# Moving gate-times-bias to GpSimd, loading the biases in rows and reordering the projection of a fused attention and feed-forward block

## What is computed

```
xn  = layernorm(x)
qkv = xn @ w_qkv.T + b_qkv              # 32 heads of 16
s   = softmax(q k^T / 4 + alibi, causal) @ v
s   = s @ w_out.T + b_out
g   = silu(ffn(xn))                     # ternary octonion weights: gate, up (1360 wide), down
out = x + s * g
```

## Time and profile before

| | |
|---|---|
| median of 3 runs | 840.68 us (839.41 to 840.71) |
| the profiled execution | 836.7 us, span 834.9 |
| TensorE busy | 796.8 us (95%) |
| VectorE busy | 631.0 us (76%) |
| ScalarE busy | 472.5 us (57%) |
| GpSimd busy | 132.6 us (16%) |
| first projection matmul | at 16.09 us |
| issue of `b_col`, of `bv_row` | at 1.25 us, at 5.11 us |
| end of the last feed-forward tile | at 402.7 us |
| first score matmul | at 406.48 us |
| granted TensorE clock | 1.2 GHz from 407.7 to 414.5 us, else 2.4 |

### The profile page before, as it was taken

The page is one execution under the profiler, slowest core; times in us unless marked ns, Lnnn a source line. Parts: engine busy times, 40 slices in busy tenths (PEclk is TensorE's granted clock), DMA queues, the critical chain, the costliest instruction groups (busy, mean ns, idle before and its releaser), DMA issues.

```text
span 834.9 us, 16148 instructions
## 1 busy us (share of the span) xinstructions
PE 796.8 (95%) x5926; PEld 350.6 (42%) x5926; DVE 631.0 (76%) x1774; ACT 472.5 (57%) x631; POOL 132.6 (16%) x183
## 2 busy tenths in 40 slices
PE   5999999999999999999899999999999999999998
PEld 3444544444444444444343343343433344343333
DVE  6656877743533565664799999999999999996546
ACT  5434285333132232222488888888888788887540
POOL 4223132223032131131000000000000003530000
PEclk9999999999999999999899999999999999999999
DMA  7474322348202201101121122222125233653635
GB/s 264 131 214 165 137 91 77 113 124 299 104 1 76 76 1 38 63 1 41 62 63 60 58 72 80 80 67 79 55 66 166 81 91 107 198 144 116 215 138 219
DMA packets 71056, 88.40 MB, mean 106 GB/s; under 512 B 26926, under 2 KB 37166, under 8 KB 70464
## 3 DMA queue, kind: packets, MB, share of 16 engines
q1 hardware_dynamic: 70848, 87.10, 32.2%
q0 software_dynamic: 128, 0.27, 0.2%
HBM read 51.15 MB, written 35.93 MB: 104 GB/s over the span
## 4 chain that ended last, share of the span: by engine, by line
PE 70%; DVE 16%; DMA 5%; issue 4%; ACT 3%; POOL 1%; SPq 0%; DVEq 0%; ACTq 0%
PE psum L1537 12%; PE psum L1494 9%; PE psum L1560 9%; PE psum L1561 9%; DVE mx L1207 8%; PE psum L1571 5%; PE psum L1572 5%; PE psum L1512 4%; DVE mshown L1203 3%; PE psum L1388 2%; PE psum L1390 2%; PE psum L1389 2%; DMA q_scr<-qk_stage 2%; PE psum L1521 2%; PE psum L1596 1%
## 5 line engine op out<-in xcount | busy, mean ns | idle before, releaser
L922 ACT ACTIVATE probs<-psum,exp_scale 128x1024 f32<-128x1024 f32 (+1 forms) x320 | 310.3, 1028 | 71.3 <-PE psum L1521 51.1
L1203 DVE CUSTOM_DVE_ANT_0 mshown<-psum,ahead 128x384 bf16<-128x384 f32 (+3 forms) x512 | 220.3, 487 | 2.8 <-PE psum L1494 0.4
L1494 PE MATMUL psum<-QKs 51*128 51x512 f16 (+3 forms) x768 | 186.2, 333 | 16.0 <-DVE mx L1207 6.3
L1537 PE MATMUL psum<-probs,Vs 128*32 128x512 f32 (+3 forms) x1536 | 162.3, 511 | 0.2 <-ACT probs L922 0.2
L1207 DVE TENSOR_REDUCE mx<-psum 128x1 f32<-128x512 f32 x256 | 157.6, 681 | 3.3 <-PE psum L1494 2.4
L1512 PE MATMUL psum<-QKs 53*128 53x512 f16 (+3 forms) x768 | 139.0, 331 | 1.6 <-ACT probs L922 1.4
L1560 PE MATMUL psum<-X,room 128*128 128x512 f16 (+1 forms) x352 | 133.6, 379 | 0.0
L1561 PE MATMUL psum<-X,room 128*128 128x512 f16 (+1 forms) x352 | 133.4, 379 | 0.0
L1494 PEld LDWEIGHTS psum<-QKs 51*128 51x128 f16 x768 | 52.1, 93 | 152.0 <-DVE mx L1203 78.9
L954 ACT ACTIVATE room<-psum,gate_half 128x512 f32<-128x512 f32 (+1 forms) x44 | 30.2, 687 | 101.2 <-PE psum L1561 101.2
L800 POOL TENSOR_TENSOR room<-room 128x512 f16<-128x512 f32 (+1 forms) x44 | 50.9, 1156 | 172.2 <-ACT room L959 172.2
(11 more groups left out here) (162 smaller groups left out, 922.1 us busy)
## 6 DMA issues: line engine op xcount, KB each, us to landing
o_scr<-osum SPq DMA_DIRECT2D x32, 256.0 KB, 3.2
QKs<-q_scr SPq DMA_DIRECT2D x96, 64.0 KB
QKs<-k_scr SPq DMA_DIRECT2D x96, 64.0 KB
q_scr<-qk_stage SPq DMA_DIRECT2D x16, 256.0 KB, 2.4
k_scr<-qk_stage SPq DMA_DIRECT2D x16, 256.0 KB, 2.2
v_scr<-v_stage SPq DMA_DIRECT2D x16, 256.0 KB, 2.1
Vs<-v_scr SPq DMA_DIRECT2D x16, 256.0 KB
probs<-in_L_attn_x SPq DMA_DIRECT2D x4, 1024.0 KB, 11.6
```

Of the source, the lines that this page charges most:

```text
L922: nc.scalar.activation(probs[n % PSLOTS][:, 2 * pair:2 * pair + 2, 0:COLS[n]], s_bank[pair][:, :, 0:COLS[n]], ACT.Exp, scale=exp_scale[:, ...
L1203: last = nc.vector.tensor_tensor_reduce(out=mshown[tiles_read(at) % 2][:, cols], in0=m_bank[bank][:, cols], in1=ahead[:, CH - keys:], scal ...
L1494: last = nc.tensor.matmul(tile[:, hh, :], Qs[s][rows, pair + hh, qb * P:(qb + 1) * P], Ks[s][rows, pair + hh, k0:k0 + keys], start=(hh == ...
L1537: last = nc.tensor.matmul(pv_bank[32 * h:32 * h + 32, CH - cols:CH], Vs[s][:, kb, h::QH], probs[n % PSLOTS][:, h, at:at + cols], start=(kb ...
```

## The change

Six edits:

1. y is made by GpSimd. VectorE scales `bo_row` once by `down_half`; then, per token tile, GpSimd multiplies `g_stage` by `bo_row` and adds x. VectorE waits, before it writes a `g_stage` buffer again, for the product of two tiles before.
2. The bias comes as 12 rows of 128, TensorE transposes it into bank 7, ScalarE copies it to `b_col` and takes its squares ahead of the first root. `bv_row` is issued by SyncE behind the weight loads.
3. GpSimd waits for the first normalisation before the three memsets.
4. In the projection: the squares of the value weights ahead of four weight pieces on ScalarE; their sum on TensorE after tile 1, not 2; the scales of the output weights at tile 1, not 2, of the second chunk; the normalisation of the second chunk one to two tiles sooner, its root at tile 2, not 4; in the third chunk the placements of w_down after tiles 2, 3, 5, 6, not 4 to 7.
5. The first batch of maximum tiles in the feed-forward stage holds one tile, not three, so that the last has three, not four; the batches in between are cut accordingly.
6. In the first quad the first score tile stands ahead of the maximum tiles.

```diff
-        if due - given >= MRING or n + 1 == len(tiles):
+        if due - given >= (MRING if given else len(early) % MRING or MRING):
...
+        if t == 0:
+            pieces.sort(key=lambda w: w != ("scores", 0, 0, 0))
...
+        DOWN_AT = [2, 3, 5, 6]
...
-        LN_AT = [[2, 3, 4, 5, 6], [2, 3, 4, 5, 6], [1, 2, 2, 3, 4]]
-        ROOT_AT = [4, 4, 2]
+        LN_AT = [[1, 2, 2, 3, 4], [2, 3, 4, 5, 6], [1, 2, 2, 3, 4]]
+        ROOT_AT = [2, 4, 2]
...
+            sp.dma_start(bv_row[:], b_qkv[2 * D:3 * D].partition_broadcast(P)).then_inc(bv_loaded, 16)
             next_x(1)
...
-            pool.dma_start(b_col[:], b_qkv.rearrange("(t p) -> p t", p=P), allow_slow_non_contiguous=True).then_inc(bias_loaded, 16)
+            pool.dma_start(b_rows[:], b_qkv.rearrange("(t p) -> t p", p=P)).then_inc(bias_loaded, 16)
...
+            pool.wait_ge(ln_step, LN_STEPS)
             for i in range(SLOTS):
                 nc.gpsimd.memset(Vs[i][:, :, QH * HD:], 1.0 / QK_SCALE).then_inc(v_ones, 1)
...
+            def gate_bias(j, t):
+
+                d = j * TT + t
+                if d == 0:
+                    pool.wait_ge(bo_ready, 1)
+                if d >= 2:
+                    pool.wait_ge(y_stored[d % 2], d // 2 * 16)
+                pool.wait_ge(f_evac, j * FTILES + 2 * HT + t + 1)
+                nc.gpsimd.tensor_tensor(y_stage[d % 2], g_stage[d % 2], bo_row[:], ALU.mult).then_inc(y_step, 1)
+                if t == 0:
+                    pool.wait_ge(x_rows_loaded[j], 16)
+                pool.wait_ge(y_step, d + 1)
+                nc.gpsimd.tensor_tensor(y_stage[d % 2], y_stage[d % 2], x_rows[j][:, t, :], ALU.add).then_inc(y_done, 1)
...
+            act.wait_ge(bias_turned, 1)
+            nc.scalar.activation(b_col[:], banks[7][:, 0:3 * KT], ACT.Copy).then_inc(bias_copied, 1)
+            act.wait_ge(bias_copied, 1)
+            for i in range(3):
+                at = SQUARES[i][1] - 1
+                nc.scalar.activation(bsquares[:, i * KT:(i + 1) * KT], b_col[:, i * KT:(i + 1) * KT], ACT.Square, accum_out=wsum[:, at:at + 1]).then_inc(squared, 1)
             root_of(0)
...
             squares(1)
+            squares(2)
             for kt in range(KT):
                 high_weight(KT + kt)
-            squares(2)
...
-                    if c == 2 and m >= NTT:
-                        place_down(m - NTT)
+                    if c == 2 and m in DOWN_AT:
+                        place_down(DOWN_AT.index(m))
...
-                    if c == 1 and m == 2:
+                    if c == 1 and m == 1:
                         out_scales()
...
+                if d == 0:
+                    dve.wait_ge(bo_loaded, 16)
+                    nc.vector.tensor_scalar(bo_row[:], bo_row[:], down_half[:, 0:1], None, ALU.mult).then_inc(bo_ready, 1)
                 if d >= 2:
                     dve.wait_ge(g_stored[d % 2], d // 2 * 16)
+                    dve.wait_ge(y_step, d - 1)
                 nc.vector.scalar_tensor_tensor(out=g_stage[d % 2], in0=held, scalar=1.0, in1=f_bank(tile), op0=ALU.add, op1=ALU.mult).then_inc(f_evac, 1)
-                if d == 0:
-                    dve.wait_ge(bo_loaded, 16)
-                if d >= 2:
-                    dve.wait_ge(y_stored[d % 2], d // 2 * 16)
-                dve.wait_ge(f_evac, tile + 1)
-                nc.vector.scalar_tensor_tensor(out=y_stage[d % 2], in0=g_stage[d % 2], scalar=down_half[:, 0:1], in1=bo_row[:],
-                                               op0=ALU.mult, op1=ALU.mult).then_inc(y_step, 1)
-                if t == HT:
-                    dve.wait_ge(x_rows_loaded[j], 16)
-                dve.wait_ge(y_step, d + 1)
-                nc.vector.tensor_tensor(y_stage[d % 2], y_stage[d % 2], x_rows[j][:, t - HT, :], ALU.add).then_inc(y_done, 1)
...
             pe.wait_ge(s_const, IDENTITY)
+            pe.wait_ge(bias_loaded, 16)
+            nc.tensor.transpose(banks[7][:, 0:3 * KT], b_rows[:], identf[0:3 * KT, 0:3 * KT]).then_inc(bias_turned, 1)
...
-                    if c == 0 and m == 2:
+                    if c == 0 and m == 1:
                         sum_squares(2)
-                    if c == 1 and m == 2:
+                    if c == 1 and m == 1:
                         sum_squares(3)
```

17 lines of the change are left out of this document (10 added, 7 removed).

## The result

The changed kernel takes 831.04 us (median of 4 runs, 829.66 to 832.83) against 840.04 for the one before (838.57 to 840.71): ratio 0.990, 95% interval 0.987 to 0.992, so 9.0 us less (intervals in brackets behind a ratio are 95% intervals throughout). Two repetitions gave 831.16 against 840.24 (0.989, 0.987 to 0.991) and 831.16 against 839.38 (0.990, 0.987 to 0.993). The direction was as forecast; the size was not: 835.7 was forecast, and 831.04 lies under the range of 832.6 to 839.3.

The account below looks back on a forecast made before the run. TensorE bounds the fourth chunk and feed-forward, VectorE's maxima the attention; only start, holes and handover can move. 1.2 + 0.7 + 1.6 + 0.9 + 0.6 = 5.0 us off the 840.68 median: 835.7 us, range 832.6 to 839.3.

Parts of the forecast that it names:

- the handover: From feed-forward to attention, 403 to 432 us: VectorE rid of y, two more maximum tiles to read; 0.6 us gained.
- the memsets: GpSimd's memsets put behind the first normalisation: VectorE's small operations beside them held at most 0.9 us; taken as nothing.
- the start: Before the projection: bias squares ahead of the root, x and W landing sooner; 1.2 us gained, from 0.8 lost to 1.9 gained.
- The 0.38 for the bias squares: At the start, VectorE's idle for the sum of the bias squares goes, as they precede the root: 0.38 us gained.
- The 0.8: At the start, x and W land sooner with bv_row's 256 KB out of the way: 0.8 us, bounds 0 and 1.5.
- rival (e): At the start, the extra table load drains ScalarE, 1.4 us once: 837.1 us, chance 0.05.
- (c): At the start, the bias rows land late, at 8.4: start 2.1 us lost, 839.0 us in all; chance 0.06.
- (d): At the start, the bias rows land later still, from 12 us on: 1.7 us slower, say 843; chance 0.03.
- First chunk: Projection to 57 us: three TensorE holes close, but a value tile's wait for a store catches up; 0.7 us gained.
- Second chunk: Projection, 60 to 95 us: output-weight scales one tile sooner close two TensorE holes; 1.6 us gained, bounds 0.8 and 1.8.
- Third chunk: Projection, 95 to 126 us: a w_down placement ahead of the root shortens the 1.74 hole; VectorE becomes last; 0.9 us gained.
- Feed-forward: Fourth projection chunk and feed-forward, 126 to 403 us: GpSimd gains 37 us of work, TensorE hides it; nothing gained or lost.

Follow-up runs that it names:

- same_after: The changed kernel once more, nothing altered, for a second profile and a closer time: 831.16 us.
- w_out_later: The changed kernel with the 1 MB load of w_out moved behind the second value store of the first chunk: 831.04 us, 0.988 of the kernel before.
- only_y: The kernel before with only y moved to GpSimd: 837.77 us against 840.24, ratio 0.997.

## Why the prediction was wrong, step by step

The medians of the single parts add up to the whole: edit 2 1.8, edit 4 3.1, edits 1, 5, 6 2.6, edit 3 on top of the new start 1.4, together 8.9 of 9.0 us. The prediction had 1.2, 3.2, 0.6 and 0, together 5.0. Each of the measured ones is uncertain by about 1.3, so that they come to 9.0 so closely is luck. Of the 4.0 us that the prediction lacks, 2.0 are the handover, where nothing was expected behind the second quad's start, 1.4 the memsets, put at nothing for a wrong reason, and 0.6 the start.

**The memsets: the step that failed, and the one with a cause shown.** "I take nothing, since a memset reads no SBUF tile and the cast was beside an operation that reads two." The question was which VectorE operations can be held, not what GpSimd reads. The row that decided was in the profile shown, four normalisations in 2.32 instead of 1.91 us. And the value was at the edge of a race: 0.32 us or less decided whether 1.6 us of wait appear. An edit whose cover is 0.3 us in one execution, with landings that scatter by 2 us, cannot be put at nothing. The Trainium skill, SBUF — State Buffer, Who interferes with whom, says it: `tensor_scalar` can enter a two-port mode, contends with GpSimd in it, and the second to issue is blocked for the whole instruction of the first. I cited that section, with the two-port mode, and used only its clause on two SBUF inputs. The runs agree with the clause that I left out: the blocked operations are TENSOR_SCALAR and end within 0.05 us of the memsets, and in the profile shown of before four operations of other kinds on 128x4 elements, two inputs in SBUF among them, ran beside the memsets at their usual 0.16 to 0.18 us (8.82 to 9.58). That last part is what my clause says. One thing goes beyond the page: the operation waited for the whole row of memsets, 1.44 us, and not for one instruction of 0.5.

**The start: near in size, wrong in the carrier.** 1.2 predicted, 1.8 measured. The 0.38 for the bias squares was right in kind; 0.56 in the two profiles above. The 0.8 was put on the landings, through bv_row's 256 KB. Where the operation on the variances runs into the memsets, as in the two profiles above, the landings of x and W do not count but the end of the memsets does, and the shorter issue of the rows brings that 0.5 us forward; bv_row alone shows no clear difference (0.6, between 1.7 gained and 0.4 lost). That the table load is hidden held (8.40 and 8.50 for the root, and 8.65 in same_after, later than 8.6 only because x landed later; in w_out_later it came 0.61 behind the load, so the drain of rival (e) is not there). Rivals (c) and (d) did not occur either. Two slips in the working changed nothing: 4.4 + 0.4 + 0.2 + 0.66 + 1.28 is 6.9 and not 7.2, and rival (e), which takes 0.8 off the start, should stand at 836.5 and not 837.1.

**First chunk: right in the end, not in the detail.** Of the three holes the one of 0.68 stayed (0.89 at 33.38). "A later wait catches up", with about 2 us just in front of the second chunk released by the split of x: 2.42, 1.82 and 2.06 in the three profiles. The gain up to there was 0.35 in the mean (41.47 to 41.12), 0.7 predicted. Not foreseen: the 1 MB load of w_out is what makes that landing late, and the hole can take the clock with it.

**Second chunk:** 1.6 predicted; 1.28 from 36.60 (mean of five) to 35.32, or 0.4 lost in the execution with the clock down. **Third chunk:** 0.9 predicted, 1.69 measured (36.92 to 35.23). I let VectorE be the last at 1.1 us later; its value tile and split were in time, and only 0.05 us of hole stayed. The sum of edit 4 came out right, 3.1 against 3.2, since these misses cancel.

**Feed-forward: right.** Nothing lost with 38 us more on GpSimd.

**Handover: the largest miss,** 0.6 predicted, 2.6 in the medians, of which only_y alone has 2.5. The profiles show 1.0 up to the second quad (301.93 to 300.94) and 1.0 from there to the last (339.04 to 338.08). The first is near the prediction: with the clock alike it is 0.8 to 0.9, 1.2 saved by y (1.5 predicted) and 0.4 lost to the two more maximum tiles (1.1 predicted), perhaps since TensorE was doing the first scores meanwhile. The step that failed is that nothing was expected behind the second quad's start. Of the second 1.0, some 0.6 is the stretch at 1.2 GHz in quad 10, which falls to a kernel by chance in so few profiles; the rest is small excesses of single quads over 23.91. The remaining 0.6 of the 2.6 are in no profile. So half of this term stays open. That the clock falls again at the handover held: 0.50 from 404.6 to 411.4 in after.

**The base of the sum.** The terms were read in one execution of before that was 4 us under its median, and that difference was added as a constant. It was not one: part of it was the first matmul at 16.09 instead of 17.8, which two of the edits remove. The six profiles with the old start show it; one could not. Of the 9.0 us, the profiles account for 6.8 when each stretch is averaged over the profiles that have an edit and those that lack it (2.35 start, 0.35, 0.94, 1.69, 1.95 from the fourth chunk to the last quad, less 0.5 in the tail). The remaining 2 lie in executions that no profile shows: the profiled ones of before are 2.1 under their medians in the mean, those of after 1.3 above theirs. What else scatters there stays open.

## What to carry to other kernels

Where the profile shows an event that just missed a wait (0.3 us here), price the edit that removes the wait by both sides of the race, missed and caught; a second profile of the kernel before is worth more than a finer reading of the first. A large load in a queue of stores that pace an engine belongs behind the stores with a due time, but a transfer moved out of one link of a chain must not stand in front of the next. Two chains of nearly equal length at a start hide each other: edit 2 alone gave 1.8, edit 3 alone nothing, and edit 3 gave about 1.4 once edit 2 was there.

## What was not expected of the hardware

A VectorE TENSOR_SCALAR on 128x4 elements took up to 1.59 us instead of 0.17 beside GpSimd memsets, which read nothing. A column of 1536 single elements, 6 KB, lands late itself (5.7 to 7.8 us, the same bytes in 12 rows 3.0 to 3.7) and keeps GpSimd 1.27 us with its issue instead of 0.72. x's fourth 256 KB tile, on another queue, landed at 7.2 to 9.4 in the eight profiles with it and at 5.9 to 7.3 in the ten without; what links the two was not tested. And the granted clock fell behind the same hole of 0.80 us in one execution and not in another, at 1.25 us for most of them.
